# Reflector steps of a small eigenproblem: three TensorE products a step in place of five, signs and gate on VectorE, the next row from one wide operation and a pair scalar

## What is computed

```
degv = A.sum(0) + A.sum(1) - diagonal(A);  Ln = D^-1/2 (diag(degv) - A) D^-1/2
_, U = eigh(Ln)                              # 120 x 120, once
f = relu(layernorm(x))                       # each of 128 samples
h = relu(U-aggregated f @ W1 + b1);  o = h @ W2 + b2
z = BN(softmax-attention over 1024 x 512 positions of o) + o
out = x + (U z) + z
```

## Time and profile before

| what | value |
|---|---|
| median of three runs | 3402.96 us (3400.95 to 3403.89) |
| profiled execution, its own time | 3405.65 us |
| its span in the profile | 3403.3 us |
| TensorE busy, over the span | 3233.0 us, 95% |
| VectorE busy | 2276.5 us, 67% |
| ScalarE busy | 2412.2 us, 71% |
| GpSimd busy | 1952.5 us, 57% |
| TensorE on the chain that ended last | 81% of the span |

### The profile page before, as it was taken

One profiled execution on the slowest core, in us unless ns is written; L12 is line 12 of the kernel. 1 busy time (PEld: TensorE's weight loads), 2 busy tenths in 40 slices (PEclk: granted clock), 3 DMA queues, 4 the chain that ended last, 5 costly groups with the idle time before them and its releaser, 6 DMA issues.

```text
span 3403.3 us, 66508 instructions
## 1 busy us (share of the span) xinstructions
PE 3233.0 (95%) x16512; PEld 2604.2 (77%) x16512; DVE 2276.5 (67%) x5891; ACT 2412.2 (71%) x4381; POOL 1952.5 (57%) x2070
## 2 busy tenths in 40 slices
PE   7888887779999999999999999999999999999997
PEld 5677776667777777777777777777777777777775
DVE  6777779636666666666666666666666666666664
ACT  5777799957666666667666676666666667667665
POOL 4333310126666666666666666666666666666665
PEclk9999999989999999999999999999999999999998
DMA  3233333412222222222222222222222222222222
GB/s 87 79 86 88 89 100 105 112 41 71 70 70 74 72 70 70 72 77 73 70 70 75 71 70 70 72 78 72 70 72 75 70 70 70 75 77 71 70 73 67
DMA packets 111578, 256.27 MB, mean 75 GB/s; under 512 B 47500, under 2 KB 49797, under 8 KB 111493
## 3 DMA queue, kind: packets, MB, share of 16 engines
q1 hardware_dynamic: 111493, 255.25, 27.2%
...
## 4 chain that ended last, share of the span: by engine, by line
PE 81%; DVE 8%; ACT 4%; issue 4%; POOL 3%; DMA 0%; DVEq 0%; POOLq 0%; ACTq 0%
PE ps_M L797 8%; PE ps_M L798 8%; PE ps_M L799 8%; PE ps_S L874 7%; PE ps_E L797 7%; PE ps_O L797 7%; PE ps_O L799 7%; PE ps_E L798 7%; PE ps_E L799 7%; PE ps_O L798 7%; PE ps_M L858 3%; ACT junkx L537 1%; PE ps_m L696 1%; POOL sc L450 1%; ACT junkx L527 1%
## 5 line engine op out<-in xcount | busy, mean ns | idle before, releaser
L503 POOL TENSOR_TENSOR p_lo<-p,p_hi 128x512 fp32r<-128x512 f32 x1024 | 1380.7, 1348 | 932.8 <-ACT p_hi L655 930.5
L650 ACT ACTIVATE p<-ps_E 128x512 f32<-128x512 f32 x1024 | 613.6, 599 | 333.2 <-PE ps_E L799 308.3
L1392 DVE TENSOR_REDUCE nmx<-ps_S 128x1 f32<-128x512 f32 x1024 | 658.7, 685 | 127.3 <-PE ps_S L874 124.0
L655 ACT ACTIVATE p_hi<-p 128x512 fp32r<-128x512 f32 x1024 | 647.2, 632 | 32.7
L797 PE MATMUL ps_E<-o_hi,Q_hi 123*128 123x512 f32 x1024 | 427.3, 417 | 0.0
L797 PE MATMUL ps_O<-p_hi,v_hi 128*121 128x512 f32 x1024 | 407.2, 398 | 4.5 <-POOL p_lo L503 4.5
L799 PE MATMUL ps_O<-p_lo,v_hi 128*121 128x512 f32 x1024 | 406.8, 397 | 0.0
L798 PE MATMUL ps_E<-o_hi,Q_lo 123*128 123x512 f32 x1024 | 404.7, 395 | 0.0
L798 PE MATMUL ps_O<-p_hi,v_lo 128*121 128x512 f32 x1024 | 404.4, 395 | 0.0
L799 PE MATMUL ps_E<-o_lo,Q_hi 123*128 123x512 f32 x1024 | 404.4, 395 | 0.0
L1372 DVE TENSOR_REDUCE gf<-ps_M 128x256 f32<-128x512 f32 x256 | 177.1, 692 | 262.0 <-PE ps_M L799 262.0
...
## 6 DMA issues: line engine op xcount, KB each, us to landing
rbc<-r_dram SPq DMA_DIRECT2D x128, 484.0 KB
xin<-in_x_dram SPq DMA_DIRECT2D x128, 480.0 KB, 4.2
xt<-in_x_dram SPq DMA_DIRECT2D x128, 480.0 KB, 4.9
out_dram<-y SPq DMA_DIRECT2D x128, 480.0 KB, 3.7
o_hi<-mrow SPq DMA_DIRECT2D x256, 2.0 KB
dcol<-y SPq DMA_DIRECT2D x128, 4.0 KB, 2.0
r_dram<-rcol SPq DMA_DIRECT2D x128, 4.0 KB, 1.4
...
```

Source lines behind the costliest of these rows:

```text
L503: pool.tensor_tensor(p_lo[:, c % 4, :], p[:, c % 4, :], p_hi[:, c % 4, :].bitcast(F32), ALU.subtract).then_inc(plo_sb, 1)
L650: act.activation(p[:, c % 4, :], ps_E[c % 2][:, :], ACT.Exp).then_inc(p_sb, 1)
L655: act.activation(p_hi[:, c % 4, :], p[:, c % 4, :], ACT.Copy).then_inc(phi_sb, 1)
L1392: dve.tensor_reduce(nmx[:, c:c + 1], ps_S[SBANK[c]][:, :], AX.X, ALU.max, negate=True).then_inc(max_sb, 1)
```

## The change

TensorE's two first products become one: the tile `XI` holds the column xcol next to the identity, 33 columns of it are the weights, and the product puts z's part in partition 0 of `ps_V` and the matrix row in partition 32. The update products get one column more (`zs` has a 1.0 in front), so that c comes out as column 0 of `ps_up`; VectorE copies it into `wyCT`, and the product that kept c and ScalarE's later copy are gone. Sign and gate are made by VectorE (`sign()`) behind the update of QA, and GpSimd only takes the root. The sign is multiplied into the row. The scaled reflector is formed before w, with the gate's factor in it, and w is made from it. For the next reflector, a wide operation reads z and the row in PSUM, two small ones form a scalar PAIR, and a second wide one makes u. The normalisation is cut into twelve units a sample (four of two transposes, eight of one product), seven to a step, three of them behind the update product. Samples of the grid count and of the factor products are 81 and from 81 on. Four small DMAs of SyncE go ahead of a wait.

```diff
-            xcol = eb("xcol", [N, 2])
+            XI = eb("XI", [N, N + 32])
             u = eb("u", [1, N])
             cs = eb("cs", [1, 2, 2 * N])
             srow = eb("srow", [1, 128])
             row1 = eb("row1", [1, N])
+            zt = eb("zt", [1, N])
             rown = eb("rown", [1, N])
-            zw = eb("zw", [1, N])
+            zs = eb("zs", [1, 2 * N])
...
+            for t, v in ((ident, 0.0), (strict, 1.0), (sub, 0.0), (ones, 1.0), (u, 0.0), (zs, 0.0), (XI, 0.0), (rstd, 1.0)):
...
+            chain(pool.memset(zs[:, N - 1:N], 1.0))
             chain(pool.affine_select(out=ident[:, :], in_=ident[:, :], compare_op=ALU.not_equal, fill=1.0,
                                      base=0, pattern=[[-1, 128]], channel_multiplier=1))
+            chain(pool.tensor_copy(XI[:, 32:N + 32], ident[0:N, 0:N]))
...
             def shift(k):
 
-                pool.wait_ge(u_ready, k + 1)
-                chain(pool.tensor_scalar(sc[:, SGN:SGN + 1], u[:, 1:2], 0.0, 2.0, ALU.is_ge, ALU.mult))
-                chain(pool.tensor_scalar(sc[:, SGN:SGN + 1], sc[:, SGN:SGN + 1], -1.0, None, ALU.add))
                 pool.wait_ge(s2_ready, k + 1)
-                chain(pool.tensor_tensor(sc[:, ROOT:ROOT + 1], sc[:, S2:S2 + 1], sc[:, 11:12], ALU.pow))
-                pool.tensor_tensor(sc[:, DU:DU + 1], sc[:, SGN:SGN + 1], sc[:, ROOT:ROOT + 1], ALU.mult).then_inc(du_ready, 1)
-                pool.tensor_scalar(sc[:, GATE:GATE + 1], sc[:, XN:XN + 1], TINY, -1.0, ALU.is_gt, ALU.mult).then_inc(gate_ready, 1)
+                pool.tensor_tensor(sc[:, ROOT:ROOT + 1], sc[:, S2:S2 + 1], sc[:, 11:12], ALU.pow).then_inc(root_ready, 1)
...
             def reflect(k, placed, wanted):
                 L = N - k
                 par = k % 2
                 cu = cs[:, par, N - k:2 * N - k]
                 pe.wait_ge(a_ready, k + 1)
-                mm(ps_row[:, k:N], ident[0:N, k + 1:k + 2], QA[:, k:N], start=True, stop=True).then_inc(row_ready, 1)
                 pe.wait_ge(xcol_ready, k + 1)
-                mm(ps_y[:, k:N], xcol[:, par:par + 1], QA[:, k:N], start=True, stop=True).then_inc(y_ready, 1)
+                mm(ps_V[0:33, 0:L], XI[:, k + 1:k + 34], QA[:, k:N], start=True, stop=True).then_inc(ry_ready, 1)
                 behind = max(placed, wanted - LN_BEHIND)
                 for i in range(placed, behind):
                     norm_piece(i)
                 pe.wait_ge(w_ready, k + 1)
-                mm(ps_up[0:N, k:N], cu, zw[:, k:N], start=True, stop=False)
-                mm(ps_up[0:N, k:N], zw[:, :], cu[:, k:N], start=False, stop=True).then_inc(up_ready, 1)
-                mm(ps_V[0:N, 128 + k:129 + k], cu, ones[0:1, 0:1], start=True, stop=True).then_inc(c_kept, 1)
+                late(pe, c_kept, k)
+                mm(ps_up[0:N, 0:L + 1], cu, zs[:, N - 1:N + L], start=True, stop=False)
+                mm(ps_up[0:N, 0:L + 1], zs[:, N - k:2 * N - k], cs[:, par, N - 1:N + L], start=False, stop=True).then_inc(up_ready, 1)
...
+            T(XI[:, 1:2], QA[:, 0:1], strict[:, 0:1], ALU.mult).then_inc(xcol_ready, 1)
...
+            def sign():
+
+                i_ge = did(TS(s_(SGN), u[:, 1:2], 0.0, 2.0, ALU.is_ge, ALU.mult))
+                did(TS(s_(GATE), s_(XN), TINY, -2.0, ALU.is_gt, ALU.mult))
+                need(i_ge)
+                return did(TS(s_(SGN), s_(SGN), -1.0, None, ALU.add))
+
             dve.tensor_copy(u[:, 1:N], QA[0:1, 1:N]).then_inc(u_ready, 1)
             dve.wait_ge(u_ready, 1)
             norm(N)
-
-            def reflect(k):
+            signed = sign()
+
+            def reflect(k, signed):
                 L = N - k
                 par = k % 2
                 cu = cs[:, par, N:2 * N]
-                dve.wait_ge(row_ready, k + 1)
-                i_row = did(dve.tensor_copy(row1[:, k:N], ps_row[:, k:N]))
-                dve.wait_ge(du_ready, k + 1)
-                i_u = did(T(u[:, 1:2], s_(DU), u[:, 1:2], ALU.add))
-                dve.wait_ge(y_ready, k + 1)
+                dve.wait_ge(ry_ready, k + 1)
+                need(signed)
+                i_row = did(TS(row1[:, k:N], ps_V[32:33, 0:L], s_(SGN), None, ALU.mult))
+                dve.wait_ge(root_ready, k + 1)
+                i_u = did(STT(out=u[:, 1:2], in0=s_(ROOT), scalar=s_(SGN), in1=u[:, 1:2], op0=ALU.mult, op1=ALU.add))
                 need(i_row)
-                i_z = did(STT(out=zw[:, k:N], in0=row1[:, k:N], scalar=s_(DU), in1=ps_y[:, k:N], op0=ALU.mult, op1=ALU.add))
+                i_z = did(STT(out=zt[:, 0:L], in0=row1[:, k:N], scalar=s_(ROOT), in1=ps_V[0:1, 0:L], op0=ALU.mult, op1=ALU.add))
                 need(i_u)
                 i_uu = did(STT(out=srow[:, k:k + 1], in0=u[:, 1:2], scalar=u[:, 1:2], in1=s_(XN), op0=ALU.mult, op1=ALU.add))
-                need(i_z)
-                i_dot = did(STT(out=sqj[:, 0:L], in0=u[:, 0:L], scalar=1.0, in1=zw[:, k:N], op0=ALU.mult, op1=ALU.mult,
-                                accum_out=s_(AC)))
                 need(i_uu)
                 i_rec = did(dve.reciprocal(s_(REC), srow[:, k:k + 1]))
-                dve.wait_ge(gate_ready, k + 1)
+                need(i_z)
+                i_dot = did(STT(out=sqj[:, 0:L], in0=u[:, 0:L], scalar=0.5, in1=zt[:, 0:L], op0=ALU.mult, op1=ALU.mult,
+                                accum_out=s_(AC)))
                 need(i_rec)
-                i_rg = did(T(s_(RG), s_(REC), s_(GATE), ALU.mult))
-                need(i_rg)
-                i_ac = did(T(s_(AC), s_(AC), s_(RG), ALU.mult))
-                late(dve, c_kept, k - 1)
-                i_cu = did(TS(cu[:, 0:L], u[:, 0:L], s_(RG), 2.0, ALU.mult, ALU.mult))
-                need(i_ac)
-                STT(out=zw[:, k:N], in0=u[:, 0:L], scalar=s_(AC), in1=zw[:, k:N], op0=ALU.mult, op1=ALU.add).then_inc(w_ready, 1)
+                i_cu = did(TS(cu[:, 0:L], u[:, 0:L], s_(REC), s_(GATE), ALU.mult, ALU.mult))
+                need(i_cu)
+                need(i_dot)
+                STT(out=zs[:, N:N + L], in0=cu[:, 0:L], scalar=s_(AC), in1=zt[:, 0:L], op0=ALU.mult, op1=ALU.add).then_inc(w_ready, 1)
                 if k + 1 < STEPS:
-                    need(i_cu)
+                    i_pair = did(STT(out=s_(PAIR), in0=cu[:, 1:2], scalar=s_(AC), in1=zt[:, 1:2], op0=ALU.mult, op1=ALU.add))
+                    i_part = did(STT(out=rown[:, 0:L - 2], in0=zt[:, 2:L], scalar=cu[:, 1:2], in1=ps_V[32:33, 2:L],
+                                     op0=ALU.mult, op1=ALU.add))
+                    need(i_pair)
+                    i_pair = did(STT(out=s_(PAIR), in0=cu[:, 1:2], scalar=s_(AC), in1=s_(PAIR), op0=ALU.mult, op1=ALU.add))
+                    need(i_part)
+                    need(i_pair)
                     dve.wait_ge(w_ready, k + 1)
-                    need(did(STT(out=rown[:, k + 2:N], in0=zw[:, k + 2:N], scalar=cu[:, 1:2], in1=row1[:, k + 2:N],
-                                 op0=ALU.mult, op1=ALU.add)))
-                    STT(out=u[:, 1:L - 1], in0=cu[:, 2:L], scalar=zw[:, k + 1:k + 2], in1=rown[:, k + 2:N],
+                    STT(out=u[:, 1:L - 1], in0=cu[:, 2:L], scalar=s_(PAIR), in1=rown[:, 0:L - 2],
                         op0=ALU.mult, op1=ALU.add).then_inc(u_ready, 1)
                     dve.wait_ge(u_ready, k + 2)
                     norm(L - 1)
                     dve.wait_ge(up_ready, k + 1)
-                    STT(out=xcol[:, 1 - par:2 - par], in0=ps_up[0:N, k + 1:k + 2], scalar=QA[:, k + 1:k + 2],
+                    STT(out=XI[:, k + 2:k + 3], in0=ps_up[0:N, 2:3], scalar=QA[:, k + 1:k + 2],
                         in1=strict[:, k + 1:k + 2], op0=ALU.add, op1=ALU.mult).then_inc(xcol_ready, 1)
                     dve.wait_ge(xcol_ready, k + 2)
                 dve.wait_ge(up_ready, k + 1)
-                T(QA[:, k:N], QA[:, k:N], ps_up[0:N, k:N], ALU.add).then_inc(a_ready, 1)
+                T(QA[:, k:N], QA[:, k:N], ps_up[0:N, 1:L + 1], ALU.add).then_inc(a_ready, 1)
+                if k + 1 < STEPS:
+                    signed = sign()
+                dve.tensor_copy(wyCT[0:N, k:k + 1], ps_up[0:N, 0:1]).then_inc(c_kept, 1)
+                return signed
...
-XN, S2, ROOT, GATE, SGN, REC, DU, RG, AC = range(9)
-LN_RATE, LN_LEAD, LN_BEHIND = (39, 10), 2, 1
-GRID_AT = 87
-WY_SLOT, WY_STEPS = 92, 19
-WY_T, WY_G = 1, 4
+XN, S2, ROOT, GATE, SGN, REC, PAIR, AC = range(8)
+UNITS = 12
+LN_RATE, LN_LEAD, LN_BEHIND = (7, 1), 2, 3
+GRID_AT = 81
+WY_SLOT, WY_STEPS = 80, 19
+WY_T, WY_G = 1, 3
```

More of the change, by code:

```diff
@@ L396, in chain @@
                 pool.wait_ge(pool_step, n[0])
-            for t, v in ((ident, 0.0), (strict, 1.0), (sub, 0.0), (ones, 1.0), (u, 0.0), (zw, 0.0), (rstd, 1.0)):
+            for t, v in ((ident, 0.0), (strict, 1.0), (sub, 0.0), (ones, 1.0), (u, 0.0), (zs, 0.0), (XI, 0.0), (rstd, 1.0)):
                 chain(pool.memset(t[:, :], v))
@@ L574, in factor @@
                 if i == 0:
[L575 to L577 removed]
+                    return
+                if i == 1:
                     act.wait_ge(wy_ps, WY_T)
```

(35 more changed lines are left out.)

22 lines of the change are left out of this document (7 added, 15 removed).

## The result

The changed kernel takes 3484.6 us (median of four runs, 3480.9 to 3488.9) against 3402.5, also of four with the profiled one; the ratio is 1.0242, 95% interval 1.0224 to 1.0260. Slower, as forecast, but by 82 us and not by 47, and above the range's end of 3467. The profiled execution took 3488.2 us (span 3486.5; before 3405.65 and 3403.3).

A forecast was written before the change was run, and what follows sets the result against it. Reflector steps between VectorE and TensorE, then ScalarE's samples, were taken to bound the setup, TensorE the steady stage. Steps +19 and samples +28 gave +47 us, 3449 us; own range 3432 to 3464, 8-in-10 range 3404 to 3467.

The forecast's parts named there:

- Two parts of the setup, and the rest equal: Setup is 117 reflector step periods, then ScalarE's slots for samples still open; the TensorE-bound steady stage stays equal.
- The samples left over, +28: After the steps: 7.6 more samples at 4.31 us, 32.7 us, less 5 back; +28 us (24 to 33).
- The grid count's wait: After the steps, TensorE's 8.5 us wait for VectorE's grid count falls to 2 us or less.
- rival 3: Reflector steps: TensorE, idle more, gets clock 0.50 in 40 more steps; +16 us, 3465; chance 0.07.
- A step at half clock, 4.2 us: Reflector step at clock 0.50: 20 matmuls take 4.0 us, some 4.2 with the chain's waits, against 3.78.
- Held starts, +0.16 a step and +19 in all: Reflector steps: four VectorE starts held by PSUM partition changes; step 3.78 for 3.62 us, +19 us (+6 to +29).
- rival 1: Reflector steps: partition quarter costs nothing; step 3.40 us, -0.22 each, -26 us; kernel 3405, no change; chance 0.15.
- The same over all lengths: Reflector steps: the middle step's +0.16 us taken for all 117 periods, long and short operands evening out.
- Rivals 1 and 2: Reflector steps without holding; the second adds sign work vanishing behind the product: step 3.32 us, kernel 3392; chances 0.15, 0.08.
- The addition: Whole kernel: 19 + 28 = +47 us, stated as 3449 us against the median of the three runs.

The follow-up runs named there:

- e1: Changed kernel with the normalisation pace of the kernel before (39 pieces in 5 steps, twelve a sample); 3448.1 us, ratio 1.012.
- e2: Changed kernel with the row again at partition 0 of PSUM, two products in place of the merged one; 3438.1 us, ratio 1.0091.
- g1: Changed kernel, merged product and row at partition 32 kept, with 9 normalisation pieces a step; 3376.6 us, ratio 0.9910.
- f3: Changed kernel with the row at partition 0 (two products) and 9 normalisation pieces a step; 3336.6 us, ratio 0.9804.
- f4: Kernel before with only its pace slowed to 7 of its pieces in 2 steps, as many samples a step as the change; 3479.7 us, ratio 1.0208.

## Why the prediction was right in direction and wrong in size

- *Two parts of the setup, and the rest equal*: right. The steady stage changed by 2 us.
- *The samples left over, +28*: right, +26.9 measured. The grid count's wait fell from 8.5 to 1.0 us, as reckoned.
- *The clock*: this is the step that failed and that put the result outside the range. The sum's term for the step has no clock in it: it is the difference of two steps at full clock, while the mean of 3.89 us in the earlier trace rows already held 13.5 us of lost time, so the forecast kept the old loss silently, and TensorE's shortened queue was priced at nothing. I had the clock as rival 3, with +16 us at a chance of 0.07 and the sentence that fewer passes make each such step cheaper. Measured: 39.1 us lost where it was 13.5, +25.6, in 53 of the 117 periods where it was 15 (periods over 0.3 us above the shortest of their k). Without these 25.6 us the median would be 3459, inside the range. At the pace of the kernel before (e1) the new step loses 29.9, so 16.4 of the 25.6 come with the new step and 9.2 with its slower pace.
- *A step at half clock, 4.2 us*: they last 4.4 to 5.2. The estimate counted TensorE's passes as one sum, and missed that the pieces behind the update then stand in front of the merged product (0.80 behind QA in the rows above).
- *Held starts, +0.16 a step and +19 in all*: the mechanism is right for three of the four starts, and e2 and g1 show it; the row's is not shown. The middle step is right to 0.04 us (0.20 longer at k = 73), part of it by luck. The forecast held that the step would be 0.22 shorter without holding (rival 1) and that holding costs 0.38; beside f3's step the three starts and the longer xcol cost 0.33, which leaves 0.13 for the shortening. Both were too large, and they partly cancel.
- *The same over all lengths*: +28.3 measured for +19. The sentence that failed is "a longer operand makes the held starts dearer and a short one cheaper, so for 117 periods with middle lengths near this one". The new step is 0.36 longer at k = 20 (4.39 against 4.03) and 0.14 at k = 100, but the held starts cost the same at both. What changes with the length is what is saved. In the old step u waits for GpSimd only where the product and the row are short. At k = 20 and at k = 100, in the kernel before:

```profile
100.48 0.25 DVE L1002 COPY row<-ps_V 1x100 f32<-1x100 f32 x1 [0.42 <-PE ps_V L715]
100.69 0.15 DVE L1004 TENSOR_TENSOR u<-sc,u 1x1 f32<-1x1 f32 x1
...
405.50 0.17 DVE L1002 COPY row<-ps_V 1x20 f32<-1x20 f32 x1 [0.30 <-PE ps_V L715]
405.94 0.15 DVE L1004 TENSOR_TENSOR u<-sc,u 1x1 f32<-1x1 f32 x1 [0.27 <-POOL sc L451]
```

From the row to u it was 0.21, 0.36 and 0.44 us at k = 20, 73 and 100, and is 0.24, 0.18 and 0.15 in the new step (g1): the shorter way through GpSimd gives 0.29 late, 0.18 in the middle and nothing early. The sum took the middle's saving for all 117 steps. One early step should have been worked out too.

- *Rivals 1 and 2, no holding*: out. With the row at partition 0 the new step is worth 2.5 us over the old one in all, not 26 or 35, and its leftover samples and clock still make it 3438.
- *The addition*: 3402.96 and 47 are 3450, one more than the 3449 that was stated; nothing hangs on it.

The 83 us between the spans are thus 28 for the longer step at full clock, 26 lost mostly to the clock, 27 for the samples, 2 elsewhere. The clock's part and the samples' are not independent, since one pace sets both: f4 shows that the slower pace by itself, in the old step, loses more to the clock than the change did.
